# Attention phase of a transformer block: SyncE issues the loads of the next token rows and context rows ahead of the store of the normalised rows

## The chip, the cores and the metric

The kernel runs on one core of a Trainium2 chip. The time is the device time of one execution in microseconds (us). The kernel before took 7116.78 us, the median of 3 runs (7114.62 to 7140.23).

The engines are named as in the profile: PE is TensorE (matmuls), DVE is VectorE, ACT is ScalarE, POOL is GpSimd, and SP is SyncE, which does no arithmetic here and issues DMAs. Each engine works through its own list of instructions in order and waits on semaphores.

## What is computed

For x and ctx of shape (4, 1024, 1024), 4096 rows in all:

```
xq  = quant_dequant_fp8(layernorm(x), blocks of 1 x 128)
wq  = quant_dequant_fp8(ctx, blocks of 128 x 128)
x1  = x + einsum('emk,enk->emn', xq, wq)        # four batches, 1024 x 1024 x 1024 each
h   = layernorm(x1)
out = x1 + mixture_of_experts(h) + shared_ffn(h) # 32 experts, 6 of them for each row
```

The first three lines are the attention phase. The blocks of ctx are 128 x 128, so their scale needs a maximum over 128 partitions. The mixture of experts and the shared FFN follow and are by far the longer part.

## The kernel before

Rows are worked on in tiles of 128 rows: TT = 32 tiles of x, 32 tiles of ctx, BT = 8 tiles in a batch. The attention phase is a software pipeline written out by hand, in which every engine has its own loop over i (a tile of x) and works on several tiles at a time. The lead of a tile is fixed: in turn i the row tile i + LEAD (LEAD = 3) of x is normalised and quantised, and the ctx tile i + CLEAD (CLEAD = 10) is quantised.

A first loop of 8 turns quantises the ctx tiles of batch 0 alone. Then the turns of x begin. Turn i of each engine:

- **SP**: `stores(i)` and then the loads. `store_x1(i)` (L317) waits for the residual of tile i, `load_res(i + 1)` (L313) fetches the rows for the next residual, and `store_x2(i)` (L321) waits on `x2_ready`, which POOL's `low_of_x2(i)` (L492) sets. After it `load_q(X, i + 4)` and `load_q(CTX, i + 11)` (both L309) wait on `qin_free`, which DVE sets when the quantising product (L1086) has read the one input buffer of its kind. `store_xt(i - 1)` (L325) is last. In the last turns of x there is no ctx load, and from turn 24 SP also loads pieces of the shared weights (L291, L292, L300).
- **DVE** (`beside`, L1196): `residual(i)` (L1130 and the statistics of x1, L1107 to L1111), then `x_moments(i + 3)` (the same lines, on the loaded rows; waits for the x load), `x2_scale(i)` (L1138, L1139; waits for ACT's std_l, L847), `x_scale(i + 3)` (L1119, L1121), `ctx_max(i + 10)` (L1050; waits for the ctx load), and `quantise` (L1053 to L1100) of tile i + 3 of x and i + 10 of ctx, with the operations of the expert choice for tile i - 2 dealt in between. In `quantise` comes x_max (L1046), then "safe" of x (L1072), then "safe" of ctx, which waits for POOL's maximum over the partitions, and only then the products L1086.
- **POOL** (`beside`, L494): `dequantise(X, i + 2)` and `dequantise(CTX, i + 9)` (L478 and L480 each), `all_max(i + 10)` (L471 waits for `ctx_max`, L472 is PARTITION_ALL_REDUCE), `low_of_nat(X)` and `low_of_nat(CTX)` (L487 twice), `low_of_x2(i)` (L492).
- **ACT**: takes PE's transposes out of PSUM (L814), takes roots (L839, L847), normalises (L843, L852) and converts to f16 (L835, L857).
- **PE**: attention products into ps_d, transposes (L627), logits.

Turns 0 to 21 hold a ctx tile for POOL's L472; turns 22 and later do not. From turn 23 POOL also splits pieces of the shared weights (L462, L463, L465).

Of the kernel before, what the change touches and what calls it, by code (L numbers as in the profile page):

```python
# [38 lines left out]
TT = T // P  # L39
# [49 lines left out]
def build(nc, x, ctx_in, gate_w, w_gate, w_up, w_down, sw_gate, sw_up, sw_down, out):  # L89
# [11 lines left out]
    with ExitStack() as stack:  # L101
# [153 lines left out]
        X, CTX = 0, 1  # L255
        LEAD = 3
        CLEAD = BT + 2
# [19 lines left out]
        def set_of_x2(i):  # L277
            return X_SETS - TT + i if isinstance(i, int) and i >= TT - 2 else i * 2 + 3
# [7 lines left out]
        def _(sp):  # L286
            def load_piece(o, c, gate, up, down):

                st = stage_of(o, c)
                if c < KH:  # L290
                    sp.dma_start(stage[:, st, 0:M], gate[c * P:(c + 1) * P, :]).then_inc(stage_in[st], 16)  # L291
                    sp.dma_start(stage[:, st, M:2 * M], up[c * P:(c + 1) * P, :]).then_inc(stage_in[st], 16)  # L292
                else:
                    r0 = (c - KH) * P
                    for h in range(2):
                        if c < CHUNKS - 1:
                            to, source = stage[:, st, h * 512:(h + 1) * 512], down[r0:r0 + P, h * 512:(h + 1) * 512]
                        else:
                            to, source = stage[h * M_LAST:(h + 1) * M_LAST, st, 0:H], down[r0:M, :]
                        sp.dma_start(to, source).then_inc(stage_in[st], 16)  # L300
# [6 lines left out]
            def load_q(kind, i):  # L307
                sp.wait_ge(qin_free[kind], i + 1)
                sp.dma_start(qin[kind], (x_rows, c_rows)[kind][ds(i * P, P), :]).then_inc(qin_in[kind], 16)  # L309

            def load_res(i):
                sp.wait_ge(x1_free, i + 1)
                sp.dma_start(xres, x_rows[ds(i * P, P), :]).then_inc(xres_in, 16)  # L313

            def store_x1(i):
                sp.wait_ge(x1_free, i + 2)
                sp.dma_start(rows_x1[ds(i * P, P), :], x1b).then_inc(x1_out, 16)  # L317

            def store_x2(i):
                sp.wait_ge(x2_ready, i + 2)  # L320
                sp.dma_start(rows_x[ds(i * P, P), :], x2nat.rearrange("p a d -> p (a d)")).then_inc(x2_out, 16)  # L321

            def store_xt(i):
                sp.wait_ge(tr_free, set_of_x2(i) + 2)
                sp.dma_start(cols_x[ds(i * P, P), :], xT_pair[:, 0, :, :].rearrange("p k n -> p (k n)")).then_inc(xt_out, 16)  # L325
# [11 lines left out]
            load_q(X, LEAD)  # L337
            load_q(CTX, CLEAD)

            def stores(i):  # L340
                store_x1(i)
                if not isinstance(i, int) or i < TT - 1:
                    load_res(i + 1)
                store_x2(i)

            stores(0)
            load_q(X, LEAD + 1)
            load_q(CTX, CLEAD + 1)
            with sp.Fori(1, TT - CLEAD - 1) as i:
                stores(i)  # L350
                load_q(X, i + (LEAD + 1))
                load_q(CTX, i + (CLEAD + 1))
                store_xt(i - 1)
            with sp.Fori(TT - CLEAD - 1, TT - CLEAD + 1) as i:
                stores(i)
                load_q(X, i + (LEAD + 1))
                store_xt(i - 1)
            for i in range(TT - CLEAD + 1, TT):
                stores(i)
                store_xt(i - 1)  # L360
                if i < TT - LEAD - 1:
                    load_q(X, i + (LEAD + 1))
                c = STAGES + i - (TT - CLEAD + 1)
                sp.wait_ge(conv_done, c - STAGES + 1)
                load_piece(0, c, *half_a)
# [1038 lines left out]
```

## Time and profile before

| what | value |
|---|---|
| median of 3 runs | 7116.78 us |
| time of the profiled execution | 7115.12 us |
| its span, first to last instruction | 7113.4 us |
| mean granted clock of TensorE | 0.964 of full speed |
| PE busy | 6460.4 us, 91% |
| POOL busy | 3385.2 us, 48% |
| DVE busy | 1619.6 us, 23% |
| ACT busy | 1032.1 us, 15% |

The span is the stretch in which the profiler saw instructions; the time holds a little more around it. The busy shares are averages over stages of quite different kinds: PE is near full only after the attention phase. An instruction that waits is not busy, and for a library operation of POOL the time in which its code is made ready shows as idle time with the releaser "issue".

### The profile page before, as it was taken

To read this page: it belongs to the slowest core of one execution; us is meant where nothing else is said; L and a number is where in the kernel's file an instruction comes from. 1 tells how busy PE (TensorE), PEld (TensorE's weight loads), DVE (VectorE), ACT (ScalarE), POOL (GpSimd) and SP (SyncE) were. 2 spreads that over 40 slices of the span, in tenths; PEclk is the share of its full clock that TensorE was granted. 3 is DMA by queue.
4 is the path that set the end of the run, shared out by engine and by line. 5 is a ranking of instruction groups with operands and counts; after the bars stand their busy time and mean duration, and the time that the engine had idled before them with its cause. 6 is when DMAs were issued, how large, how long until landed. Compare 5 with 4: busy or idle time off the path is not lost.

```text
span 7113.4 us, 89519 instructions
## 1 busy us (share of the span) xinstructions
PE 6460.4 (91%) x32678; PEld 3079.8 (43%) x32679; DVE 1619.6 (23%) x2586; ACT 1032.1 (15%) x1206; POOL 3385.2 (48%) x2190
## 2 busy tenths in 40 slices
PE   0554577999999999999999999999999999999998
PEld 0232333444444444444444444444444444444444
DVE  3555584001111111111111111111111111114555
ACT  1333341111111111111111111111111111110000
POOL 3454575445433555336543464355546446533222
PEclk9777788999999999999999999999999999999999
DMA  1222344998555556555555565555656555649877
GB/s 52 86 99 96 106 150 154 340 336 287 151 137 138 152 153 166 137 137 159 155 152 143 141 166 154 139 152 154 166 141 167 153 141 163 168 117 259 260 257 224
DMA packets 1146756, 1175.21 MB, mean 165 GB/s; under 512 B 867296, under 2 KB 867296, under 8 KB 1146720
## 3 DMA queue, kind: packets, MB, share of 16 engines
q10 hardware_dynamic: 902352, 477.20, 28.5%
q1 hardware_dynamic: 184464, 487.80, 21.0%
q0 software_dynamic: 59904, 209.75, 8.1%
q8 instruction: 20, 0.33, 0.0%
q14 instruction: 16, 0.13, 0.0%
HBM read 647.63 MB, written 327.16 MB: 137 GB/s over the span
## 4 chain that ended last, share of the span: by engine, by line
PE 81%; issue 8%; DMA 4%; POOL 4%; DVE 3%; ACT 0%; SPq 0%; POOLq 0%; ACTq 0%; DVEq 0%
PE ps_gu L636 53%; PE ps_d L636 24%; POOL wts L487 2%; PE ps_d L739 2%; DMA hT<-hid_hl 2%; DMA wts<-in_x 2%; PE ps_d L737 2%; POOL wts L492 1%; POOL wts L478 0%; DVE amax_p L1050 0%; DVE stats_q L1108 0%; DVE wts L1284 0%; POOL wts L480 0%; SPq L321 0%; ACT wts L843 0%
## 5 line engine op out<-in xcount | busy, mean ns | idle before, releaser
L636 PE MATMUL ps_gu<-wts,xT 128*128 128x512 f16 (+1 forms) x19584 | 3929.7, 362 | 9.2 <-DVEq L1324 4.0
L636 PEld LDWEIGHTS ps_gu<-wts,xT 128*128 128x128 f16 x19584 | 1894.8, 98 | 2040.0 <-issue 121.2
L636 PE MATMUL ps_d<-wts,hT 128*128 128x512 f16 x8160 | 1810.5, 380 | 26.8 <-DMA hT<-hid_hl 26.8
L462 POOL TENSOR_SCALAR wts<-stage 128x1408 f16<-128x1408 f32 (+1 forms) x476 | 588.0, 1235 | 2259.9 <-PE ps_d L739 2243.3
L1236 DVE SCALAR_TENSOR_TENSOR hid<-ps_gu,sil 128x704 f32<-128x704 f32 x272 | 242.4, 891 | 4572.7 <-ACT sil L936 4421.4
L465 POOL TENSOR_TENSOR wts<-stage,wts 128x1408 f16<-128x1408 f32 (+1 forms) x476 | 1232.2, 2589 | 39.8
L636 PEld LDWEIGHTS ps_d<-wts,hT 128*128 128x128 f16 x8160 | 799.0, 98 | 980.8 <-DMA hT<-hid_hl 21.1
L463 POOL TENSOR_SCALAR stage<-stage 128x1408 f32<-128x1408 f32 (+1 forms) x476 | 628.6, 1321 | 0.0
L936 ACT ACTIVATE sil<-ps_gu 128x704 f32<-128x704 f32 x272 | 205.9, 757 | 2844.8 <-PE ps_gu L636 2514.1
L958 ACT ACTIVATE dout<-ps_d 128x1024 f32<-128x1024 f32 x240 | 245.6, 1023 | 2176.2 <-DMA xT<-xin 1960.9
L627 PE MATMUL ps_t<-ident,wts 128*128 128x128 f16 x1024 | 88.4, 255 | 362.7 <-POOL wts L487 358.3
L636 PE MATMUL ps_d<-wts,xin 128*128 128x512 f16 x1536 | 368.7, 400 | 44.4 <-DVE wts L1130 34.2
L1243 DVE TENSOR_TENSOR hid_hl<-hid,hid_hl 128x640 f16<-128x640 f32 x272 | 299.6, 1102 | 0.0
L487 POOL TENSOR_TENSOR wts<-wts 128x1024 f16<-128x1024 f32 x64 | 171.0, 2684 | 243.0 <-issue 215.7
L942 ACT ACTIVATE hid_hl<-hid 128x704 f16<-128x704 f32 x272 | 214.9, 790 | 289.6 <-DVE hid L1236 263.2
L636 PEld LDWEIGHTS ps_d<-wts,xin 128*128 128x128 f16 x1536 | 153.5, 102 | 235.0 <-issue 44.2
L1268 DVE SCALAR_TENSOR_TENSOR wts<-wts,top_w 128x1024 f32<-128x1024 f32 x192 | 246.5, 1284 | 26.9 <-DVE wts L1265 3.3
L627 PEld LDWEIGHTS ps_t<-ident,wts 128*128 128x128 f16 x1024 | 78.6, 117 | 383.5 <-issue 325.9
L607 POOL DMA_INDIRECT wts<-rows_d,slot_now x192 | 199.8, 1041 | 76.9 <-issue 49.7
L602 POOL COPY slot_now<-slot 128x6 int32 (+1 forms) x32 | 6.0, 187 | 465.3 <-DVE wts L1268 394.3
L566 POOL DMA_INDIRECT rows_x<-wts,slot_now x192 | 187.9, 978 | 77.2 <-issue 50.9
L627 PE MATMUL ps_gu<-ident,wts 128*128 128x128 f16 x512 | 55.8, 297 | 153.4 <-POOL wts L487 153.4
(149 smaller groups left out, 2215.6 us busy)
## 6 DMA issues: line engine op xcount, KB each, us to landing
rows_d<-dout ACTq DMA_DIRECT2D x240, 512.0 KB
xin<-rows_x ACTq DMA_DIRECT2D x211, 512.0 KB, 3.3
stage<-in_L_ffn_w_down SPq DMA_DIRECT2D x384, 256.0 KB, 3.2
stage<-in_L_ffn_w_gate SPq DMA_DIRECT2D x256, 352.0 KB, 3.3
stage<-in_L_ffn_w_up SPq DMA_DIRECT2D x256, 352.0 KB, 3.9
wts<-in_x SPq DMA_DIRECT2D x64, 512.0 KB, 5.6
rows_x<-wts SPq DMA_DIRECT2D x64, 512.0 KB, 3.3
wts<-rows_x SPq DMA_DIRECT2D x64, 512.0 KB, 8.1
```

Of the source, the lines that this page charges most:

```text
L462: g.tensor_scalar(high, raw, WSCALE, 1.0, ALU.mult, ALU.mult).then_inc(conv_step, 1)
L463: g.tensor_scalar(raw, raw, WSCALE, 1.0, ALU.mult, ALU.mult).then_inc(conv_step, 1)
L465: g.tensor_tensor(low, raw, high, ALU.subtract).then_inc(conv_done, 1)
L487: g.tensor_tensor(nat[kind][:, 1, :], deq[kind], nat[kind][:, 0, :], ALU.subtract)\
L627: last = nc.tensor.transpose(to[:, a, k * P:(k + 1) * P], src[:, a, k * P:(k + 1) * P], ident[:, :])
L636: ins = nc.tensor.matmul(dst[c], left, right[c], start=(first and a == 0), stop=(last and a == 2))
L936: a.activation(sil[:, :, :].rearrange("p a c -> p (a c)"), ps_gu_flat[:, 0:M], ACT.Silu, scale=1.0 / WSCALE).then_inc(silu_done, 1)
L942: a.activation(hid_hl[:, 0:M], hid[:, :, :].rearrange("p a c -> p (a c)"), ACT.Copy)\
L958: a.activation(dout[:, :], ps_d_flat, ACT.Copy, scale=1.0 / (WSCALE * HSCALE)).then_inc(d_free, 1)
L1236: v.scalar_tensor_tensor(out=hid[:, :, :].rearrange("p a c -> p (a c)"), in0=ps_gu_flat[:, M:2 * M], scalar=HSCALE / WSCALE, in1=sil[:, :, ...
L1243: v.tensor_tensor(hid_hl[:, M + M_LAST:], flat[:, 0:K_LAST], hid_hl[:, 0:K_LAST], ALU.subtract).then_inc(hid_low, 1)
L1268: ins = v.scalar_tensor_tensor(out=total[u], in0=gat[u][:, k, :], scalar=top_w[:, ds(i, 1), k:k + 1].rearrange("p a k -> p (a k)"), in1=to ...
```

## The change

SP's turn becomes one function, `around(i)`, in which `load_q(X, i + 4)` and `load_q(CTX, i + 11)` stand behind `load_res(i + 1)` and ahead of `store_x2(i)`. The waits of each step stay what they were, and so do the buffers and all other engines. `store_xt(i - 1)` stays behind `store_x2(i)`; in the last turns the x load also moves ahead of `store_xt`. No instruction is added or taken out.

```
-            def stores(i):
+            def around(i, x=True, ctx=True, cols=True):
                 store_x1(i)
                 if not isinstance(i, int) or i < TT - 1:
                     load_res(i + 1)
+                if x:
+                    load_q(X, i + (LEAD + 1))
+                if ctx:
+                    load_q(CTX, i + (CLEAD + 1))
                 store_x2(i)
-
-            stores(0)
-            load_q(X, LEAD + 1)
-            load_q(CTX, CLEAD + 1)
+                if cols:
+                    store_xt(i - 1)
+
+            around(0, cols=False)
             with sp.Fori(1, TT - CLEAD - 1) as i:
-                stores(i)
-                load_q(X, i + (LEAD + 1))
-                load_q(CTX, i + (CLEAD + 1))
-                store_xt(i - 1)
+                around(i)
             with sp.Fori(TT - CLEAD - 1, TT - CLEAD + 1) as i:
-                stores(i)
-                load_q(X, i + (LEAD + 1))
-                store_xt(i - 1)
+                around(i, ctx=False)
             for i in range(TT - CLEAD + 1, TT):
-                stores(i)
-                store_xt(i - 1)
-                if i < TT - LEAD - 1:
-                    load_q(X, i + (LEAD + 1))
+                around(i, x=i < TT - LEAD - 1, ctx=False)
                 c = STAGES + i - (TT - CLEAD + 1)
                 sp.wait_ge(conv_done, c - STAGES + 1)
                 load_piece(0, c, *half_a)
```

## Rows read from the trace of the kernel before

**Rows 1.** Windows of two stages: core's busy us and count, granted clock, DMA.

```profile
255.00:890.00 635.00, 319.03 (x2413) 190.00 (x2411) 338.62 (x913) 230.49 (x267) 328.81 (x161) 0.74 0.29 99
925.00:1040.00 115.00, 89.43 (x624) 45.87 (x624) 102.73 (x212) 50.01 (x60) 93.24 (x40) 0.85 0.46 159
```

**Rows 2.** Chain of waits through one turn: start us, us, what.

```profile
526.41 0.04 SPq L321
...
527.15 5.50 DMA wts<-in_x
...
532.67 0.06 DVE stats_q L1107
...
535.10 1.22 DVE amax_p L1050
...
536.35 0.02 POOLq L471
...
542.35 0.05 POOL amax L472
...
549.93 5.64 POOL wts L487 x2
555.57 2.10 POOL wts L492
```

**Rows 3.** Waits of DVE, 255 to 890 us: total, times, longest.

```profile
DVE stats_q L1107 <- DMA wts<-in_x: 186.0, 20, 9.6
DVE safe L1072 <- POOL amax L472: 92.9, 21, 5.0
```

**Rows 4.** Line L472, 255 to 890 us: its instructions, and POOL's idle time before them.

```profile
L472 POOL PARTITION_ALL_REDUCE amax<-amax_p x21: 393/393/394, 262.2 to 885.2; - x21
...
  issue: 154.0, 21
```

**Rows 5.** Timeline of POOL before the steady turns: start, us, instruction, [idle before].

```profile
50.02 0.39 POOL L472 PARTITION_ALL_REDUCE amax<-amax_p  x1 [5.66 <-issue]
...
205.19 0.39 POOL L472 PARTITION_ALL_REDUCE amax<-amax_p  x1 [6.01 <-issue]
...
217.36 2.34 POOL L478 TENSOR_TENSOR wts<-wts 128x1024 f32<-128x1024 f32 x1
...
221.63 2.37 POOL L478 TENSOR_TENSOR wts<-wts 128x1024 f32<-128x1024 f32 x1
224.08 1.90 POOL L480 TENSOR_TENSOR wts<-wts,from_q 128x1024 f32<-128x1024 f32 x1
231.90 0.39 POOL L472 PARTITION_ALL_REDUCE amax<-amax_p  x1 [5.92 <-issue]
```

**Rows 6.** Timeline of all engines around the same turn, 200 to 230 us.

```profile
207.53 0.33 SPq L309 DMA_DIRECT2D wts<-in_x  x1
...
222.08 1.21 DVE L1050 TENSOR_REDUCE amax_p<-wts 128x8 f32<-128x1024 f32 x1
...
224.80 1.20 DVE L1072 TENSOR_SCALAR safe<-amax 128x8 f32<-128x8 f32 x1
```

**Rows 7.** Timeline of all engines in the steady turn of rows 2.

```profile
531.23 6.64 PE L636 MATMUL ps_d<-wts,xin 128*128 128x512 f16 x30
...
544.16 1.22 DVE L1086 TENSOR_TENSOR wts<-wts,to_q 128x1024 f32<-128x1024 f32 x1
...
549.15 2.35 DVE L1100 TENSOR_TENSOR wts<-wts 128x1024 f32<-128x1024 f32 x2
...
559.57 0.20 ACT L847 ACTIVATE std_l<-var_l 128x1 f32<-128x1 f32 x1
```

**Rows 8.** Timeline: the last turn with ctx, and one turn of the tail.

```profile
905.97 0.69 DVE L1107 BATCH_NORM_STATS2 stats_q<-wts 128x6 f32<-128x512 f32 x1 [8.64 <-DMA wts<-in_x]
...
911.91 5.18 POOL L487 TENSOR_TENSOR wts<-wts 128x1024 f16<-128x1024 f32 x2 [2.86 <-ACT wts L835]
...
967.22 0.69 DVE L1107 BATCH_NORM_STATS2 stats_q<-wts 128x6 f32<-128x512 f32 x1
```

## The prediction

> **What bounds the kernel now.** I first read the busy shares by stage, to see what kind of time the change can touch. In the attention phase PE is busy for half of the stretch and no engine is full [rows 1], so waits between engines set its length, and an engine's share says nothing. The reader should therefore look for the loop of waits that closes once a turn. The chain of waits gives it: POOL ends `low_of_x2`, SP wakes at 526.41 and issues the store, then the x load at 527.15, which takes 5.50 us; DVE starts on the loaded rows at 532.67, ends `ctx_max` at 536.32, POOL passes L471 at 536.35, starts its all-reduce at 542.35, and works without a break from 549.93 to 557.67, where SP wakes again [rows 2]. So the load is on the loop today. The waits of DVE say the same by size: 186.0 us in 20 turns, 9.3 us each, for exactly these loads, and 92.9 us for POOL's maximum [rows 3]. The 21 steady all-reduces lie from 262.2 to 885.2 us, so a turn takes 623.0 / 20 = 31.15 us [rows 4].
>
> The trap is to read the 9.3 us as the gain. The question is what POOL does meanwhile. While the load is under way POOL dequantises; its four operations take 8.6 us (217.36 to the end of L480 at 225.98 in an early turn) [rows 5]. Counted from 526.4, it is done near 535.0, and `ctx_max` ends at 536.32 [rows 2]. POOL thus loses only 1.3 us a turn to the late load. The rest of its idle time before the all-reduce, 6.0 us from 536.35 to 542.35, begins after its wait is over [rows 2]: it belongs to the operation itself.
>
> **What the change removes.** The x load is set free by L1086, which ends at 545.38, 3.0 us after the all-reduce starts, and the ctx load by the second L1086 right behind it, before 547 [rows 7]. In the early turn, where SP stood at this load already, it issued at 207.53, 2.3 us after the all-reduce at 205.19 [rows 5, 6]. With the loads ahead of L321 SP issues them there and not 12 us later. With 5.5 us for the landing both are in SBUF by about 553, before the 557.67 at which SP would only have asked for them today [rows 2].
>
> What then is late next? On DVE, `x2_scale` stands ahead of `ctx_max` and needs std_l, which ACT gives at 559.57 [rows 7]; that remains. If I put the whole stretch from the first statistics to the end of `ctx_max` (532.67 to 536.32, 3.65 us) behind it, `ctx_max` ends by 563.4 at the latest [rows 2, 7]. POOL's dequantising in that turn ends at 557.67 + 8.6 = 566.3. So POOL's wait at L471 is over 2.9 us before POOL gets there, and POOL alone sets the turn. The attention product that the next residual needs ends at 537.87, over 13 us before DVE is free of L1100 at 551.50 [rows 7], so DVE's earlier start meets no late PE.
>
> The new idle time before the all-reduce is that of turns in which `ctx_max` was done early. There is such a turn: `ctx_max` ended at 223.29, POOL's L480 at 225.98, and the all-reduce started at 231.90, 5.92 us of idle time [rows 5, 6]. Today it is 154.0 / 21 = 7.33 us [rows 4]. The term is 21 x (7.33 - 5.92) = 29.6 us. Its ends: 6.01 us in the turn before gives 27.7, and 5.66 us in the ctx-only loop gives 35.1 [rows 5]. I take 5.92, since it is the same code of POOL with the same four operations ahead.
>
> After the all-reduce nothing changes: DVE's quantising follows POOL's result, and POOL's L487 ends with it; I put 0 there.
>
> **The last ctx turn and the tail.** In the first turn without an all-reduce DVE waits 8.64 us for the load, and POOL idles 2.86 us because ACT is late behind DVE [rows 8]. The 2.86 us can go, but DVE's large operations then run next to POOL's and slow each other. I take 2.5 us, with ends of 0 and 5 us (nothing, and somewhat under twice the 2.86). In the tail DVE's first x statistics have no wait for a load [rows 8], so an earlier load there is worth nothing.
>
> **What moves past what.** Per turn two load issues move ahead of one store issue on SP's queue. The store needs POOL at 557.67 and the waits put ahead of it are over before 547, so it is not later; `store_xt` and `store_x1` behind it are asked for two load issues sooner. Cost 0, with 10 us of cover. If the cover were gone, ACT's `high_of_x2` would be what waits for the store.
>
> DVE's `ctx_max`, x_max and "safe" of x move from POOL's idle time to beside the dequantising. In the early turn just this happened: L478 took 2.37 us under `ctx_max` and 2.34 us alone, L480 kept 1.90 us, and it was "safe" that stretched to 1.20 us [rows 5, 6]. So POOL loses 0.03 us, which I leave out; as a bound, if two small operations of about 0.17 us each got ahead of POOL in every turn, 21 x 0.34 = 7.1 us would go.
>
> The Trainium skill (SBUF — State Buffer, Who interferes with whom) speaks against the change here: an f32 scalar operation or cast of DVE may take the port pair shared with GpSimd, and then the other "fully blocks", the earlier issuer winning. By that rule "safe" and the cast of the choice could hold POOL up, and the sum would be 7.1 us smaller; it says of reductions that on this chip they never contend, and the 2.37 against 2.34 us agrees [rows 5].
>
> **Sum.** 29.6 + 2.5 = 32.1 us less. The attention phase is all ahead of the expert phase, so nothing hides it. Against the profiled execution, 7115.1 - 32.1 = 7083.0 us; that execution lies 1.7 us below the median, so a median would be 7084.7 us. I say 7084.5.
>
> **The rivals.**
>
> 1. POOL-bound as above. Gain from 27.7 - 7.1 = 20.6 to 35.1 + 5 = 40.1 us: 7076.7 to 7096.2 us. Chance 0.81.
> 2. DVE's wait goes but the turn keeps its length, because POOL's idle time before the all-reduce stays at 7.3 us whatever came before, or because another input of `ctx_max` is late (std_l, if ACT slips by 3 us). For it: rows 4 show only late turns. Against it: 5.92 and 6.01 us [rows 5]. Time 7117. Chance 0.09.
> 3. DVE, not POOL, was the bound, and the waits of DVE count in full: 186.0 us, 6931 us. Against it: POOL works or readies its operation in all but 1.3 us of a turn [rows 2]. Anything well above 40 us belongs here. Chance 0.04.
> 4. Slower: DVE's reductions do hold POOL's dequantising up, or are held up by it until they are late. The place is the 8.6 us of L478 and L480; `ctx_max` and x_max at 1.2 us each make 2.4 us a turn, 21 x 2.4 = 51 us, less the 29.6: 7138 us; with two statistics of 0.69 us more, 80 us less 29.6: 7167 us. It decides from 1.4 us a turn; slower by 0.5% needs 3.1 us a turn. Against it: the early turn [rows 5, 6]. Chance 0.06.
>
> **How the numbers follow.** About 0.5% (35.6 us) is what a measurement of this kernel can tell from no change. The forecast of 32.1 us lies just under it: of case 1 I give a quarter to gains above 35.6 (0.20), with case 3 and rounding 0.26 for faster. Of case 4, 0.05 lies beyond 0.5%; with rounding I say 0.06 for slower, and 0.68 for within. Case 1's own range, 7077 to 7096, holds not quite 8 in 10 once its bounds are doubted; I widen it to 7072 to 7108, which takes in a gain of a quarter of the sum.
>
> **What would show it.** The steady turns should take near 29.75 us (21 all-reduces over 595 us); the idle time before L472 should be near 5.9 us each, some 124 us in all; the group of DVE waiting for the x load should be gone, with the time turned into waits for std_l and for POOL; SP should issue L309 ahead of L321 by about 11 us. L478 and L480 should keep 2.34 and 1.90 us. The prediction is wrong if L472's idle time stays above 7 us, if L478 grows, or if the turn falls far below 29.7 us.

## The result, and the profile after

Over 20 runs each, the changed kernel took 7099.02 us (median; 7083.06 to 7191.42) and the kernel before 7134.66 us (7112.03 to 7198.17). The ratio of the times is 0.9943, with a 95% interval from 0.9922 to 0.9964: 41 us less, and 26 to 56 us by the interval. The ratio compares means and leaves out, as slow, the one execution of 7191.42 us, while three of the kernel before above 7190 us stay in; with it in, the means differ by 36 us, as the medians do (35.6 us). The forecast was 32.1 us less.

The profiled executions are one each: span 7091.6 us after, 7113.4 us before, 21.8 us less. Where the difference lies is seen better by the point at which the attention phase is over, the first of PE's two products that rank the experts:

```profile
L703 PE MATMUL ps_gu<-wts,upper x2: 609/622/634, 1091.7 to 1092.5; 128*128 128x512 f16 x2
```

That is one tile's view of the changed kernel (count, shortest/median/longest ns, first and last start). The same view of the kernel before:

```profile
L707 PE MATMUL ps_gu<-wts,upper x2: 609/622/634, 1120.3 to 1121.1; 128*128 128x512 f16 x2
```

The attention phase ends 28.6 us sooner. The rest of the span, whose code is the same, took 7091.6 - 1091.7 = 5999.9 us after and 7113.4 - 1120.3 = 5993.1 us before; so a difference of 21.8 us between two spans is 28.6 us of effect and 6.8 us of something else.

The loop of waits of a steady turn looks like this in the changed kernel (chain of waits: start us, us, what; all line numbers behind L350 are four lower than before):

```profile
501.06 0.39 POOL amax L468
501.45 0.09 POOLq L483 x2
501.54 6.87 issue
508.41 5.88 POOL wts L483 x2
514.29 2.08 POOL wts L488
516.37 2.31 POOL wts L474
...
518.75 1.90 POOL wts L476
520.65 2.32 POOL wts L474
...
523.11 2.03 issue
...
525.19 0.90 issue
...
526.11 2.74 issue
...
529.10 1.91 issue
531.01 0.39 POOL amax L468
```

No engine but POOL is left in it, in this turn and in all the others from the first steady all-reduce to the last: in [rows 2] SP, a load and DVE stood between POOL's L492 and its next all-reduce, here POOL goes straight through. The line of the all-reduce answers to [rows 4]:

```profile
L468 POOL PARTITION_ALL_REDUCE amax<-amax_p x21: 393/393/394, 262.6 to 859.0; - x21
...
  issue: 125.4, 21
```

A turn takes (859.0 - 262.6) / 20 = 29.82 us, where it took 31.15, and POOL idles 125.4 / 21 = 5.97 us ahead of the all-reduce, where it was 7.33.

DVE's waits, 255 to 890 us, answer to [rows 3]:

```profile
DVE safe L1068 <- POOL amax L468: 175.5, 21, 8.6
DVE scale_l L1134 <- ACT std_l L843: 75.6, 21, 3.9
```

The wait for the x load, 186.0 us, is gone. But 175.5 and 75.6 us stand there now where 92.9 us stood: 251.1 - 92.9 = 158.2 us of the 186.0 only changed their names. What DVE really gained is the 28 us that the loop got shorter.

SP and DVE in the timeline of the same turn:

```profile
504.28 0.35 SPq L309 DMA_DIRECT2D wts<-in_x  x1
...
505.57 0.33 SPq L309 DMA_DIRECT2D wts<-in_ctx  x1
...
516.54 0.36 SPq L321 DMA_DIRECT2D rows_x<-wts  x1
...
517.93 0.20 ACT L843 ACTIVATE std_l<-var_l 128x1 f32<-128x1 f32 x1
...
518.82 1.21 DVE L1046 TENSOR_REDUCE amax_p<-wts 128x8 f32<-128x1024 f32 x1
...
520.61 2.37 POOL L474 TENSOR_TENSOR wts<-wts 128x1024 f32<-128x1024 f32 x1
...
521.97 1.03 DVE L1068 TENSOR_SCALAR safe<-amax 128x8 f32<-128x8 f32 x1
```

The x load is issued 12.3 us ahead of the store. `ctx_max` ends at 520.03, when POOL still dequantises, until 524.95. L474 takes 2.37 us beside x_max, and it is DVE's "safe" that stretches, as in [rows 5, 6].

### The profile page after: what moved, and what is told of

It is laid out like the page before. It is cut to its first block, busy times and chain, and to the rows that moved or that the text cites. A ratio compares the mean times of both kernels' runs of the same rounds, so it can differ in the third digit from the quotient of the medians.

```text
span 7091.6 us, 89519 instructions
## 1 busy us (share of the span) xinstructions
PE 6462.3 (91%) x32678; PEld 3073.7 (43%) x32679; DVE 1630.7 (23%) x2586; ACT 1032.3 (15%) x1206; POOL 3388.4 (48%) x2190
## 4 chain that ended last, share of the span: by engine, by line
PE 82%; issue 8%; POOL 6%; DMA 2%; DVE 2%; ACT 0%; POOLq 0%; DVEq 0%; ACTq 0%; SPq 0%
PE ps_gu L632 54%; PE ps_d L632 24%; DMA hT<-hid_hl 2%; POOL wts L483 2%; PE ps_d L735 2%; POOL wts L474 2%; PE ps_d L733 2%; POOL wts L488 1%; POOL wts L476 1%; DVE wts L1280 0%; POOL amax L468 0%; ACT wts L839 0%; DVE amax L1042 0%; POOL wts L461 0%; DVE hid L1232 0%
## 5 line engine op out<-in xcount | busy, mean ns | idle before, releaser
L483 POOL TENSOR_TENSOR wts<-wts 128x1024 f16<-128x1024 f32 x64 | 174.4, 2737 | 238.0 <-issue 213.5
L632 PEld LDWEIGHTS ps_d<-wts,xin 128*128 128x128 f16 x1536 | 153.3, 102 | 235.1 <-issue 43.1
```

The costliest lines, as they stand in the source:

```text
L483: g.tensor_tensor(nat[kind][:, 1, :], deq[kind], nat[kind][:, 0, :], ALU.subtract)\
L632: ins = nc.tensor.matmul(dst[c], left, right[c], start=(first and a == 0), stop=(last and a == 2))
```

## The experiments

Every run has one change against the kernel before or the changed kernel. The length of a turn in the trace, from the line of the all-reduce over 18 to 20 turns, tells small differences apart that the times don't: the times of one kernel lie over 100 us apart. Ratios are against the kernel before on the same chip, with the 95% interval.

**One load alone.** e1_x_only moves only the x load, e2_ctx_only only the ctx load.

```
 e1_x_only, against the changed kernel        e2_ctx_only
                 if x:                      -  if x:
                     load_q(X, ...)         -      load_q(X, ...)
-                if ctx:                       if ctx:
-                    load_q(CTX, ...)              load_q(CTX, ...)
                 store_x2(i)                   store_x2(i)
+                if ctx:                    +  if x:
+                    load_q(CTX, ...)       +      load_q(X, ...)
```

> Only the x load stands ahead of the store of the normalised rows; the ctx load stays behind it. Theory (POOL sets the turn, and the late load cost it only what POOL waited at L467/L471): the ctx load is asked for 15.9 us after the all-reduce starts and lands at about 21.5, ctx_max ends at about 22.8, POOL is ready at 23.9, so the turn stays that of the changed kernel, 29.8 to 30.2 us, and the time lies 25 to 40 us below the kernel before. Rival (the ctx load is what the turn waited for): the turn goes back to about 31.1 us and the time to that of before.

> Only the ctx load stands ahead of the store; the x load stays behind it. Theory: DVE's statistics of x stand ahead of ctx_max, so ctx_max still ends about 25 us after the all-reduce starts and POOL still waits 1.2 us for it: turn 31.0 to 31.3 us, idle time before the all-reduce 7.2 to 7.4 us, time within 10 us of before. Rival (the ctx load was the late one): turn 29.9 us.

e1_x_only, the line of the all-reduce and POOL's idle time before it:

```profile
L468 POOL PARTITION_ALL_REDUCE amax<-amax_p x20: 395/395/396, 262.9 to 829.5; - x20
...
  issue: 119.3, 20
```

The turn is 566.6 / 19 = 29.82 us and the idle time 5.97 us, both those of the changed kernel; ratio 0.9948 (0.9910 to 0.9987). So the move of the x load is enough for the whole gain.

e2_ctx_only:

```profile
L468 POOL PARTITION_ALL_REDUCE amax<-amax_p x20: 392/393/394, 263.2 to 840.3; - x20
...
  issue: 132.1, 20
```

The turn is 577.1 / 19 = 30.37 us and the idle time 6.61 us; ratio 0.9989 (0.9969 to 1.0010). The sign was as expected, the size was not: 31.0 to 31.3 us was expected, and more than half of the gain per turn is there without the x load having moved. The chain of waits of that run shows why:

```profile
520.99 0.35 SPq L321
...
521.61 4.71 DMA wts<-in_x
```

The x load is asked for 0.6 us after the store, as before, but it lands in 4.71 us and not in 5.50 [rows 2]. It is so in every turn: between 300 and 860 us it takes 4.30 to 4.76 us here (median 4.5) and took 4.95 to 5.66 us before (median 5.4). In the kernel before, the ctx load was issued 0.6 us behind it; here `store_xt` is what follows 0.6 us behind. The 0.86 us between the medians is the size of the 0.78 us by which the turn fell.

Nor is 4.7 us what the load takes by itself. In the changed kernel the x load of 504.28 us, which no store stands just ahead of, takes

```profile
DMA to landing us min/median/max: 3.3/3.3/3.3
```

and so it does in every turn (3.1 to 3.4 us), although the ctx load follows 1.29 us behind it; in e1_x_only, where the ctx load follows 12.9 us behind, it is the same 3.3 us. So of the 5.4 us before, 3.3 are the load's own, and some 2.1 us came with its neighbours: 1.2 us are still there in e2_ctx_only, between `store_x2` and `store_xt`, and 0.9 us go with the ctx load. Which of the neighbours costs what at which distance, no pair of runs takes apart.

**One more POOL operation.** In both kernels one more product on POOL of 1.9 us ahead of the all-reduce:

```
+                if kind == CTX:
+                    g.tensor_tensor(spare..., quant[kind]..., from_q[:, kind, :]..., ALU.mult)
                 g.tensor_tensor(deq[kind]..., quant[kind]..., from_q[:, kind, :]..., ALU.mult)
```

> The changed kernel with one more product on POOL (L476 for ctx once more into spare memory, 1.9 us) ahead of the all-reduce. Theory (POOL sets the turn): turn 29.9 + 1.9 = 31.8 us, idle time before the all-reduce stays near 6.0 us. Rival (DVE or a load sets it): turn stays at 29.9 us and the idle time shrinks.

> The kernel before with the same product. Theory: POOL waited 1.3 us for ctx_max, which takes up part of the 1.9 us: turn 31.15 + 0.6 = 31.75 us, the same as in the changed kernel with this product, and the gain of the change is gone. Rival (the two are independent): turn 31.15 + 1.9 = 33.0 us.

e5_after_more_pool:

```profile
L469 POOL PARTITION_ALL_REDUCE amax<-amax_p x19: 393/394/396, 281.0 to 849.2; - x19
...
  issue: 111.8, 19
```

e6_before_more_pool:

```profile
L473 POOL PARTITION_ALL_REDUCE amax<-amax_p x19: 393/394/396, 280.0 to 848.6; - x19
...
  issue: 112.3, 19
```

Turns of 31.57 and 31.59 us, idle times of 5.88 and 5.91 us. The changed kernel pays 1.75 us for the 1.9 us of work, the kernel before only 0.44, and the two orders are then the same. The ratios, 1.0027 (1.0000 to 1.0053) and 1.0051 (1.0025 to 1.0078), overlap.

**One more DVE operation** just ahead of `ctx_max`, 1.2 us:

```
+                v.tensor_reduce(amax_p[:, X, :], blocks(qin[CTX]), AX.X, ALU.max, ...)
                 v.tensor_reduce(amax_p[:, CTX, :], blocks(qin[CTX]), AX.X, ALU.max, ...)
```

> The changed kernel with one more reduction on DVE just ahead of ctx_max (1.2 us). Theory: ctx_max has some 4 us in hand, so the turn stays at 29.9 us. Rival (DVE sets the turn, or its reductions hold POOL up): 31.1 us.

> The kernel before with the same reduction. Theory: the load, DVE and POOL are one loop, so the turn takes the whole of it: 31.15 + 1.2 = 32.35 us. Rival (POOL's idle time before the all-reduce is its own in both kernels): turn 31.15 us.

e7_after_more_dve:

```profile
L468 POOL PARTITION_ALL_REDUCE amax<-amax_p x21: 393/394/397, 261.9 to 856.0; - x21
...
  issue: 123.0, 21
```

e8_before_more_dve:

```profile
L472 POOL PARTITION_ALL_REDUCE amax<-amax_p x19: 393/394/396, 264.8 to 843.9; - x19
...
  issue: 158.6, 19
```

The changed kernel takes 594.1 / 20 = 29.71 us a turn, nothing of the 1.2 us; the kernel before takes 579.1 / 18 = 32.17 us, 1.02 us more, and its idle time rises to 8.35 us. (The trace of e8 is that of its longest execution, 7238.55 us; its attention phase, from which these numbers come, ends at 1143.6 us, and the stage behind it took 6092 us, where it took 5993 in the trace of the kernel before.) Ratios 0.9963 (0.9944 to 0.9981) and 1.0015 (0.9982 to 1.0049). With the runs before it, this shows that before, DVE's work ahead of `ctx_max` was on the loop and after it is not, while POOL's is.

**Without the all-reduce.** In both kernels POOL's all-reduce becomes a copy. These two leave out the maximum over the partitions.

```
-                g.partition_all_reduce(amax[:, CTX, :], amax_p[:, CTX, :], P, ReduceOp.max)...
+                g.tensor_copy(amax[:, CTX, :], amax_p[:, CTX, :])...
```

> The changed kernel with POOL's all-reduce over the partitions replaced by a plain copy of the per-partition maxima (the ctx scales are then per row and not per block; the amount of other work is the same). Theory: without the 5.9 us before and the 6.9 us behind the all-reduce POOL's turn falls to 15 us of work, the turn falls to 20 to 24 us and DVE or PE sets it. Rival (DVE sets the turn already): the turn stays at 29 to 30 us.

> The kernel before with the same replacement. Theory: now the load is not covered by the all-reduce's idle time: 6.3 us from the store's release to the landing, 3.7 to the end of ctx_max, 8.7 of quantising, 4.1 and 2.1 of POOL, 25 us a turn, so 3 to 5 us more than the changed kernel with the same replacement, where with the all-reduce the difference is 1.2 us. Rival (the load costs the same 1.2 us a turn in any case): 1.2 us.

The residuals of e3_after_copy in the timeline of DVE, one a turn:

```profile
411.91 1.22 DVE L1125 SCALAR_TENSOR_TENSOR wts<-ps_d,wts 128x1024 f32<-128x1024 f32 x1
...
434.99 1.22 DVE L1125 SCALAR_TENSOR_TENSOR wts<-ps_d,wts 128x1024 f32<-128x1024 f32 x1
```

and in e4_before_copy, with SP's instructions between:

```profile
404.47 0.33 SPq L321 DMA_DIRECT2D rows_x<-wts  x1
...
404.82 1.22 DVE L1085 TENSOR_TENSOR wts<-wts,to_q 128x1024 f32<-128x1024 f32 x1
...
406.23 0.35 SPq L309 DMA_DIRECT2D wts<-in_x  x1
...
412.08 1.22 DVE L1129 SCALAR_TENSOR_TENSOR wts<-ps_d,wts 128x1024 f32<-128x1024 f32 x1
...
435.15 1.22 DVE L1129 SCALAR_TENSOR_TENSOR wts<-ps_d,wts 128x1024 f32<-128x1024 f32 x1
```

Both take 23.08 us a turn; ratios 0.9576 (0.9544 to 0.9609) and 0.9558 (0.9529 to 0.9588), from two executions of each. For e3 the theory held: the all-reduce with its idle time was what set the turn, and DVE, which now waits for nothing in these turns, sets it. For e4 it fell: 25 us were expected, and 3 to 5 us of difference between the orders; there is none. The mistake was to keep POOL's L487 behind DVE's quantising, which is so only where the all-reduce holds both. Without it POOL ends its turn early, SP's store is out at 404.47, and the load then waits for DVE's L1085 in either order.

**The maximum on DVE.** The runs point to a version that beats both kernels: keep the result, but take the all-reduce off POOL.

```
+                step(v.tensor_reduce(mx_in[:, 0:KH], blocks(qin[CTX]), AX.X, ALU.max, ...))
+                step(v.transpose(mx_t[:, :], mx_in[:, :]))
+                for q in range(4):
+                    mark(step, v.tensor_reduce(mx_q[:, q:q + 1], mx_t[q * 32:(q + 1) * 32, :], AX.X, ALU.max))
+                wait_last(step)
+                for q in range(4):
+                    mark(step, v.tensor_reduce(mx_all[q * 32:(q + 1) * 32, :],
+                                 mx_q[:, :].unsqueeze(1).to_broadcast([32, 32, 4]), AX.X, ALU.max))
+                wait_last(step)
+                mark(step, v.transpose(mx_out[:, :], mx_all[:, :]))
...
-                all_max(i + CLEAD)        # POOL; and the three other calls
```

> The changed kernel with the maximum over the partitions made by eleven small operations of DVE (a transpose of 32 x 32 blocks, reductions across the four groups of partitions, a transpose back) in the place of POOL's all-reduce; the result is the same. Theory: POOL no longer sets the turn; with a plain copy in its place the turn was 23.1 us and DVE's, and ten more small operations of DVE at about 0.25 us bring it to 25 to 27 us; with the shorter ctx-only loop the time lies 110 to 200 us below the kernel before. Rival (the small operations wait for the port beside POOL's, as the small scalar operations did): 30 us and more, no gain.

> The same with the loads behind the store, as in the kernel before. Theory: POOL ends the low half of the normalised rows before DVE has read the input buffers, as in the pair of runs with the plain copy, so the order on SP decides nothing: the turn within 0.2 us of that of the run with the loads ahead. Rival (the load is late again by what the order costs): turn 1.2 us longer.

e9_max_on_dve took 6891.32 us (6872.35 to 6982.70), ratio 0.9661 (0.9637 to 0.9686); e10_max_on_dve_old_order 6884.92 us (6874.31 to 6909.22), ratio 0.9657 (0.9630 to 0.9684). That is 3.4% less than the kernel before, some 240 us, where 110 to 200 us were expected. The timeline of e10, the new operations and two residuals:

```profile
443.65 1.22 DVE L1133 SCALAR_TENSOR_TENSOR wts<-ps_d,wts 128x1024 f32<-128x1024 f32 x1
...
450.39 0.21 DVE L1045 STREAM_TRANSPOSE mx_t<-mx_in 128x32 f32<-128x32 f32 x1
450.63 0.80 DVE L1047 TENSOR_REDUCE mx_q<-mx_t 32x1 f32<-32x32 f32 x4
451.47 1.20 DVE L1050 TENSOR_REDUCE mx_all<-mx_q 32x32 f32<-32x128 f32 x4
...
452.70 0.21 DVE L1053 STREAM_TRANSPOSE mx_out<-mx_all 128x32 f32<-128x32 f32 x1
...
454.84 2.05 DVE L1075 TENSOR_SCALAR safe<-amax 128x8 f32<-128x8 f32 x1
...
456.88 2.10 DVE L1075 TENSOR_SCALAR safe<-mx_out 128x8 f32<-128x8 f32 x1
...
467.33 1.22 DVE L1133 SCALAR_TENSOR_TENSOR wts<-ps_d,wts 128x1024 f32<-128x1024 f32 x1
```

The new operations run from 450.39 to 452.91, 2.5 us, but the turn is 23.69 us (443.65 to 467.33), only 0.6 us more than with the copy and below the 25 to 27 us expected. The traces show where the rest went. In e3_after_copy three small operations of DVE in each turn ended only with the POOL operation beside them:

```profile
420.91 4.22 POOL L482 TENSOR_TENSOR wts<-wts 128x1024 f16<-128x1024 f32 x2 [0.32 <-ACT wts L830]
420.95 2.11 DVE L1157 TENSOR_SCALAR chosen<-iota_e,group_f 128x4 f32<-128x4 f32 x1
...
425.09 2.13 POOL L487 TENSOR_TENSOR wts<-dout,wts 128x1024 f16<-128x1024 f32 x1
...
425.26 1.99 DVE L1164 TENSOR_SCALAR chosen<-chosen 128x4 f32<-128x4 f32 x1
```

With L1160 between them (1.98 us) that is 6.1 us in all, and the same three take 0.5 us in e10. There two are held instead, the two "safe", 4.15 us where two free ones take 0.34. So 2.5 us of new work came with some 1.8 us less of holding (5.6 against 3.8), which leaves 0.7 us, near the 0.6 us measured. The durations are the same in all turns between 300 and 600 us. Why it is two operations there and three here was not tested.

In e9 the turn is 23.69 us too (419.89 to 443.58), so the order on SP decides nothing any more, as expected. The trace of e9 is that of its longest execution (6982.70 us), but what is longer lies behind the attention phase, which ends at 872.3 us in both.

## Why the prediction was right

**What bounds the kernel.** Right. The loop POOL, SP, load, DVE, POOL was real, and it cost only what POOL waited at L471: in the kernel before, 1.9 us more on POOL cost 0.44 us (e6) and 1.2 us more on DVE cost 1.02 us (e8); in the changed kernel the same two additions cost 1.75 us (e5) and nothing (e7), so POOL alone is left.

**The steady turns**, 29.6 us forecast: POOL's idle time before the all-reduce fell by 154.0 - 125.4 = 28.6 us over the 21. A turn of 29.75 was forecast and 29.82 measured; 5.92 us of idle time, and 5.97 measured. The early turn in which `ctx_max` was done ahead of POOL [rows 5, 6] was a true picture of the changed kernel.

**The last ctx turn**, 2.5 us forecast within 0 and 5: from the last all-reduce to the end of the phase it was 1120.3 - 885.2 = 235.1 us and is 1091.7 - 859.0 = 232.7 us, 2.4 us less. The 2.86 us for which POOL waited for ACT are gone: its L483 starts at 882.89, right behind L476. The size was a choice between the two ends and not worked out, so that it came so near is luck. The tail kept its length.

**The port shared with GpSimd.** The rule of the Trainium skill (SBUF — State Buffer, Who interferes with whom) was weighed at up to 7.1 us. The trace agrees that reductions do no harm (L474 2.37 us), and of "safe" it shows that DVE was the one to wait (1.03 us), so nothing of the 7.1 us came. In the runs without the all-reduce too it was DVE's small operations that waited for POOL's, some 2 us each.

**What the sum left out.** From the first to the last steady all-reduce it was 623.0 us and is 596.4, 26.6 us less; the end gives 2.4 us more, and the first steady all-reduce came at 262.6 and not at 262.2 us, 0.4 us later: 26.6 + 2.4 - 0.4 = 28.6 us by which the phase ends sooner. The turn ahead of the first steady all-reduce had become shorter too, but the start of the phase was some 2 us later in this execution, ahead of any load that moved, and took that back.

**The sum and its chances.** 32.1 us was forecast, 28.6 us is seen in the trace, and the times say 26 to 56 us. The ratio gives 0.57%, just beyond the bound of 0.5%, and I gave gains beyond it only 0.26; the medians give 0.50%, and the interval holds both sides. The 7 to 12 us by which the times exceed the 28.6 us of the trace were not traced to anything, and the interval doesn't ask for a cause. The forecast as an absolute time was further off: 7084.5 us against 7099.02, 14.5 us too low, because it was counted from the median of 3 executions (7116.78 us), and 20 executions of the same kernel have 7134.66. That the time still lies inside 7072 to 7108 us is in part luck.

**A detail that was right for an incomplete reason.** The prediction treated the 5.50 us of the x load as its own duration. In the place to which the change moves it, it takes 3.3 us, and 4.5 us behind the store but without the ctx load (e2_ctx_only). It made no difference to the sum, since the load left the loop altogether; it is why the expectation for e2_ctx_only missed.

## What to carry to other kernels

A wait of 9.3 us a turn on DVE was worth 1.3 us, because it lay beside POOL's work: before pricing a removed wait, go round the whole loop and find which engine has no idle time but its own, then read the price from the gap at that engine alone. Look for a turn at the start of a loop in which the condition after the change already holds, since it shows the new loop and its cost to a few hundredths of a microsecond. And once the loop is down to one engine, the next step is that engine's dearest operation (here 13 us around an operation that shows as 0.39 us busy), which was worth six times the reordering and made the reordering immaterial.

## What was not expected of the hardware

A load of 512 KB that lands in 3.3 us with no store just ahead of it took 5.4 us (medians over the turns) with a store 0.6 us ahead and another load 0.6 us behind, and 4.5 us when that other load was taken away; this last step alone made 0.8 us of every turn. A load 1.29 us behind it cost it nothing.

The stage behind the attention phase, whose code is the same in these four kernels, took 5993.1 us before, 5999.9 after, 7112.2 - 1092.4 = 6019.8 in e1_x_only and 7134.0 - 1146.1 = 5987.9 in e5_after_more_pool. The attention phase ended at 1091.7, 1092.4 and 1087.8 us in three kernels with the same turn (the changed one, e1_x_only, e7_after_more_dve). So a difference of 30 us in this kernel can be read from one trace if it is read from the stage that changed, and not from the span.

In e10 the two stream transposes of 128 x 32 took 0.21 us each and the four reductions that gather the groups of 32 partitions into one 0.80 us together; with 1.20 us for the four that hand the result back this makes a maximum over 128 partitions for 8 columns in 2.5 us; POOL's all-reduce took 0.39 us by its own line and about 13 us by the gaps around it (means over the 21 steady turns of the changed kernel: 5.97 before, 7.12 behind). The gap ahead of it is in line with the Trainium skill (GPSIMD Engine Reference, Instruction dispatch), which gives some 6 us for the first call of a kernel whose code has just been loaded; the trace shows a gap of about that size twice a turn, going into the all-reduce (5.97 us) and coming back out of it (7.12 us).
